# Curvature stage: fields as 32x32 products of plain float32 from turned copies of the image, with H's numerator and the step summed on TensorE

## The reference, cut to what matters

```
sobel_x, sobel_y: 3x3 kernels / 8; ux, uy = dw(u, sobel_x), dw(u, sobel_y)
uxx, uxy, uyy = dw(ux, sobel_x), dw(ux, sobel_y), dw(uy, sobel_y)     # all five clipped to +-10
g2 = ux*ux + uy*uy;  denK = 1 + g2;  denH = sqrt(1 + g2 + 1e-6)
K = clip((uxx*uyy - uxy*uxy) / (denK*denK + 1e-6), -5, 5)
H = clip(((1+uy*uy)*uxx - 2*ux*uy*uxy + (1+ux*ux)*uyy) / (2*denH**3 + 1e-6), -5, 5)
u = u + 0.01 * clip(alpha*K + beta*H, -1, 1)
u = edge-pad of u's interior                                          # ten times
return 0.7*u + 0.3*x
```

## Time and profile before

| | us |
|---|---|
| median of 3 runs (744.8 to 745.09) | 745.0 |
| the profiled execution's own time | 745.53 |
| its span, first to last instruction | 743.7 |
| PE busy | 657.2 (88%) |
| VectorE busy | 449.9 (60%) |
| ScalarE busy | 374.2 (50%) |
| GpSimd busy | 317.2 (43%) |

### The profile page before, as it was taken

How to read it: one execution, slowest core, us unless ns; L and a number is a source line. 1 busy time by engine, 2 the same in 40 slices (tenths; PEclk the granted TensorE clock), 3 DMA queues, 4 the chain that set the end, 5 groups by cost and what they waited for, 6 DMA issues and landing times.

```text
span 743.7 us, 11210 instructions
## 1 busy us (share of the span) xinstructions
PE 657.2 (88%) x4384; PEld 462.0 (62%) x4384; DVE 449.9 (60%) x673; ACT 374.2 (50%) x630; POOL 317.2 (43%) x296
## 2 busy tenths in 40 slices
PE   6997899998974566797989999999999999999994
PEld 4784774565442334454555787777777777777782
DVE  5730000095046222132444599999999999999997
ACT  1310000060000011020224699999999999999995
POOL 1000000010013100000000689999999999999993
PEclk9999999999997889899999999999999999999997
DMA  9999999999999999999982000000000000000001
GB/s 376 427 384 423 426 428 427 427 425 425 429 425 425 427 429 424 430 425 427 428 364 97 1 2 0 1 0 0 0 0 0 0 0 0 0 0 0 0 0 57
DMA packets 13347, 166.53 MB, mean 224 GB/s; under 512 B 1456, under 2 KB 1856, under 8 KB 2944
## 3 DMA queue, kind: packets, MB, share of 16 engines
q1 hardware_dynamic: 12384, 162.60, 51.7%
q0 software_dynamic: 256, 2.02, 0.7%
q10 hardware_dynamic: 672, 1.41, 0.5%
HBM read 164.98 MB, written 1.05 MB: 223 GB/s over the span
## 4 chain that ended last, share of the span: by engine, by line
DVE 39%; DMA 27%; PE 25%; issue 6%; ACT 1%; POOL 1%; DVEq 0%; POOLq 0%; SPq 0%; ACTq 0%
DMA ring<-wout_w 15%; DVE ring L905 6%; PE bank L383 6%; DVE ring L910 5%; PE bank L399 5%; DVE ring L892 4%; DVE bank L889 4%; DVE bank L925 4%; PE bank L452 4%; PE bank L507 4%; DMA ring<-wv_p 3%; DVE bank L913 3%; DMA ring<-wout_p 3%; DVE ring L916 3%; DMA ring<-wqk_p 3%
## 5 line engine op out<-in xcount | busy, mean ns | idle before, releaser
L591 PE MATMUL bank<-u_parts,vmr 128*128 128x480 f32 x1360 | 309.0, 385 | 6.6 <-DVE reg_a L899 4.7
L591 PEld LDWEIGHTS bank<-u_parts,vmr 128*128 128x128 f32 x1360 | 249.6, 188 | 65.9 <-DVE reg_a L899 16.7
L399 PE MATMUL bank<-ring,small 128*32 128x256 f32 x1152 | 76.5, 413 | 36.2 <-DMA ring<-wout_w 30.6
L399 PEld LDWEIGHTS bank<-ring,small 128*32 128x32 f32 x1152 | 38.3, 117 | 66.2 <-issue 33.0
L399 PE MATMUL bank<-ring,xw 128*32 128x256 f32 x1024 | 60.6, 394 | 13.8 <-DMA ring<-wv_w 13.8
L1144 POOL DMA_DIRECT2D vmr<-vmats x1 | 0.5, 540 | 151.3 <-PE bank L399 151.3
L1123 POOL MEMSET reg_d<- 128x2176 f32 x1 | 1.9, 1915 | 146.8 <-PE bank L459 146.8
L720 DVE SCALAR_TENSOR_TENSOR reg_a<-bank,prm 128x512 f32<-128x512 f32 x4 | 2.8, 692 | 100.9 <-PE bank L459 100.9
L383 PE MATMUL bank<-reg_a,ring 128*128 128x256 f32 x256 | 56.2, 380 | 3.0 <-DMA ring<-wqk_p 2.3
L399 PEld LDWEIGHTS bank<-ring,xw 128*32 128x32 f32 x1024 | 33.2, 113 | 39.6 <-DMA ring<-wv_w 17.1
L383 PEld LDWEIGHTS bank<-reg_a,ring 128*128 128x128 f32 x256 | 48.3, 190 | 11.1 <-DMA ring<-wqk_p 3.1
(11 more groups left out here) (197 smaller groups left out, 1026.8 us busy)
## 6 DMA issues: line engine op xcount, KB each, us to landing
ring<-wv_w SPq DMA_DIRECT2D x32, 2048.0 KB, 29.6
ring<-wout_w SPq DMA_DIRECT2D x30, 2048.0 KB, 37.0
ring<-wqk_p SPq DMA_DIRECT2D x4, 2048.0 KB, 18.9
ring<-wqk_w SPq DMA_DIRECT2D x4, 2048.0 KB, 20.7
ring<-wv_p SPq DMA_DIRECT2D x2, 2048.0 KB, 20.5
ring<-wout_p SPq DMA_DIRECT2D x2, 2048.0 KB, 22.9
ring<-wout_w SPq DMA_DIRECT2D x4, 1024.0 KB, 35.5
vmr<-vmats POOLq DMA_DIRECT2D x1, 1664.0 KB, 6.9
```

Of the source, the lines that this page charges most:

```text
L399: ins = te.matmul(bank[32 * j:32 * j + 32, b_, n0:n0 + 256], lhs(c), slot[k % NSLOT][:, c, 256 * j:256 * j + 256], start=start and c == 0, ...
L591: last = te.matmul(dst[:, 0:NF], mat(m, first), p3[:, 2 + off:S + off, :], start=(high and n == 0), stop=(not high and n == len(terms) - 1))
```

## The change

The float32r split is gone: ScalarE's high parts, GpSimd's low parts and their buffers. A term is now a plain float32 product in 32x32 tiles of the array: four matmuls, one for each row quarter, each with its own output quarter. A chunk now has its channels on quarters of 32 partitions (one channel's 32 rows), so the operator matrix is 32x32. The terms of uy, uxy and uyy/uxx read copies of the image turned by 1, 2, 3 quarters (`turned`; uxx uses the copy turned by 1), so that fields of different turns use different tiles; the output comes out in place. SyncE makes the three copies of a chunk with six DMAs, SBUF to SBUF, after every update (`turn`).

TensorE also forms sums that other engines formed: H's numerator as a + b - 2 cross (three sets of four tiles with unit and -2 matrices) and the step as alpha dt K + beta dt H (two sets). VectorE loses L925 (combining K and H) and L932 (the cross product); L905 becomes two products of 480 (K's, H's). ScalarE's joint 960-wide log and exponential are split into halves, and the Relu clips are two, not three. GpSimd forms the cross product, clips K (a tensor_scalar), and no longer makes the low part, the sum of outers or the final sum of H. TensorE's and GpSimd's programs are written out rather than looped.

The way in also changes: the first 24 columns go to HBM (eight DMAs) and back (four) in the chunk layout, and the last 8 columns are turned by 64 products with a selection matrix. `vmats` is smaller, and SyncE loads it and `select`.

```diff
-            p.dma_start(vmr[:, :], vmats).then_inc(ld_vm, 16)
+            sp.dma_start(vm[:, 0:ALPHA * S], vmats).then_inc(ld_vm, 16)
+            sp.dma_start(sel, select).then_inc(ld_sel, 16)
+            for r in range(RG):
+                sp.dma_start(to[:, :, r, :], xa4[r * C:(r + 1) * C, :, 1:1 + EARLY, :]).then_inc(st_image, 16)
+            sp.wait_ge(st_image, 16 * RG)
+            for x in range(NCH):
+                sp.dma_start(u_half(x, 0), image[x * P:(x + 1) * P, :]).then_inc(ld_u[x], 16)
+            def turn(c):
+                for t in range(1, NCH):
+                    cut_ = QUAD * t
+                    sp.dma_start(turned[cut_:P, t - 1, c, :], u[c][0:P - cut_, :]).then_inc(ld_turn[t - 1][c], 16)
+                    sp.dma_start(turned[0:cut_, t - 1, c, :], u[c][P - cut_:P, :]).then_inc(ld_turn[t - 1][c], 16)
...
+                for c in range(NCH):
+                    sp.wait_ge(po["pad"], i * NCH + (c + 1 - NCH))
+                    turn(c)
...
+            def stencil(field, c, t, first, terms, n):
+                for j in range(NCH):
+                    at_ = slice(QUAD * ((j + t) % NCH), QUAD * ((j + t) % NCH + 1))
+                    last = te.matmul(bank[QUAD * j:QUAD * (j + 1), field, 0:NF], mat(m, (j + t) % NCH), whole[at_, 2 + off:S + off, :],
...
+            def slot_step(k):
+                    if older:
+                        te.wait_ge(ve["khk"], k - 2)
+                        te.wait_ge(ve["khh"], k - 2)
+                    stencil(ux, c, 0, first, UX, 0)
+                    te.wait_ge(ld_turn[0][c], 32 * (i + 1))
+                    stencil(uy, c, 1, first, UY, 0)
+                    stencil(ux, c, 0, first, UX, 1)
+                    stencil(uy, c, 1, first, UY, 1)
+                    te.wait_ge(ld_turn[1][c], 32 * (i + 1))
+                    if old:
+                        te.wait_ge(ve["clipxy"], k - 1)
+                    stencil(uxy, c, 2, first, UXY, 0)
+                    te.wait_ge(po["clip_k"], k - 2)
+                    add(STEP, ALPHA, clip_k[q], True, False)
+                    stencil(uy, c, 1, first, UY, 2).then_inc(pe["fld1"], 1)
+                    stencil(uxy, c, 2, first, UXY, 1)
+                    te.wait_ge(ld_turn[2][c], 32 * (i + 1))
+                        te.wait_ge(ve["clip2"], k - 1)
+                    stencil(uyy, c, 3, first, UYY, 0)
+                    te.wait_ge(ac["clip_h"], k - 2)
+                    add(STEP, BETA, clip_h[q], False, True).then_inc(pe["step"], 1)
+                    stencil(uxx, c, 1, first, UXX, 0)
+                    stencil(uxy, c, 2, first, UXY, 2)
+                    stencil(uyy, c, 3, first, UYY, 1)
+                    te.wait_ge(ve["outer"], k - 1)
+                    add(h_sum, ONE, ab[n][:, 0:NF], True, False)
+                    stencil(uxx, c, 1, first, UXX, 1)
+                    stencil(uxy, c, 2, first, UXY, 3).then_inc(pe["fldxy"], 1)
+                    stencil(uyy, c, 3, first, UYY, 2)
+                    add(h_sum, ONE, ab[n][:, NF:2 * NF], False, False)
+                    stencil(uxx, c, 1, first, UXX, 2)
+                    stencil(uyy, c, 3, first, UYY, 3)
+                    te.wait_ge(po["cross"], k - 1)
+                    add(h_sum, MINUS_TWO, cross[n], False, True).then_inc(pe["hn"], 1)
+                    stencil(uyy, c, 3, first, UYY, 4).then_inc(pe["fld2"], 1)
```

VectorE's order in a slot becomes: clip1 (960, as L892), clipd (as L889) and, directly behind and dependent on it, u (as L899); khk (480), clipxy (as L913), khh (480), clip2 (960, as L910), slope (as L916), outer (960, as L920):

```diff
+                    v.wait_ge(pe["step"], k - 2)
+                    v.tensor_scalar(step, step, five_ab[:, 1:2], DT, ALU.subtract, ALU.min).then_inc(ve["clipd"], 1)
+                    v.wait_ge(ve["clipd"], k - 2)
...
-                    v.tensor_tensor(two(kh[n]), two(num[n]), fields_in(n, 0, 2), ALU.mult).then_inc(ve["kh"], 1)
+                    v.wait_ge(ac["invk"], k - 1)
+                    v.tensor_tensor(kh[n][:, 0:NF], num[n], pair(n)[:, 0, :], ALU.mult).then_inc(ve["khk"], 1)
...
+                    v.wait_ge(pe["hn"], k - 1)
+                    v.wait_ge(ac["invh"], k - 1)
+                    v.tensor_tensor(kh[n][:, NF:2 * NF], pair(n)[:, 1, :], inv_h[n], ALU.mult).then_inc(ve["khh"], 1)
```

More of the change, by code:

```diff
@@ L134 @@
 EDGE_BANK = (3, 4, 0, 1)
-NVM = 2 * len(MATS) * P
+MIXED, OUTER, STEP = 2, 3, 7
+ONE, MINUS_TWO, ALPHA, BETA = range(2 * len(MATS), 2 * len(MATS) + 4)
+NVM = (BETA + 1) * S
+TURNS = NCH - 1
+SEL = 2 * S - RG
 def build(nc, x_patch, x_window, x_conv, params, wqk_p, wv_p, wout_p, wqk_w, wv_w, wout_w,
-          conv_band, conv_halo, vmats, edge, out):
+          conv_band, conv_halo, vmats, edge, select, image, out):
     with ExitStack() as ctx:
@@ L222, in build @@
             "pl_sq_sums", "pln", "negmax", "prob", "pf", "dsl", "stage", "conv", "bank_turn", "img",
-            "clip1", "clipxy", "clip2", "slope", "outer", "cross", "kh", "diff", "clipd", "u", "scales", "fin", "halo", "u_in", "band")}
+            "clip1", "clipxy", "clip2", "slope", "outer", "khk", "khh", "clipd", "u", "scales", "mats", "fin", "halo", "u_in", "band")}
         ac = {n: sem("ac_" + n) for n in (
             "order", "patch_sq", "patch_std", "fl", "win_sq", "win_std", "pl_std", "qkv", "vt", "exp", "pt", "rows",
-            "wwk", "wv", "conv", "p2", "sqr", "sqxy", "lnw", "psq", "w15", "lnd", "inv", "end_k", "up_h", "ends", "x3", "hi", "hi_first", "halo", "u_in")}
-        po = {n: sem("po_" + n) for n in ("zero", "bandz", "pick", "padz", "lo", "lo_first", "cxy", "m", "num", "absum", "hn", "pad")}
+            "wwk", "wv", "conv", "p2", "sqr", "sqxy", "lnw", "psq", "w15", "lnk", "lnh", "invk", "invh", "low_h", "clip_h", "x3",
+            "halo", "u_in")}
+        po = {n: sem("po_" + n) for n in ("zero", "bandz", "padz", "cxy", "m", "num", "cross", "clip_k", "pad")}
+        st_image, ld_u = sem("st_image"), [sem(f"ld_u{c}") for c in range(NCH)]
+        ld_turn = [[sem(f"ld_turn{t}_{c}") for c in range(NCH)] for t in range(1, NCH)]
         ld_last, st_out = [sem(f"ld_last{n}") for n in range(NPIECE)], sem("st_out")
@@ L269, in build @@
         dual = lambda cols: [arena(cols) for _ in range(2)]
-        u_hi = [u_parts[:, c * ROWF:(c + 1) * ROWF] for c in range(NCH)]
-        u_lo = [u_parts[:, (NCH + c) * ROWF:(NCH + c + 1) * ROWF] for c in range(NCH)]
+        vm, sel = arena(NVM), arena(C * SEL)
+        turned = arena(TURNS * NCH * ROWF).rearrange("p (t c n) -> p t c n", t=TURNS, c=NCH)
         u_in = lambda c: u[c][:, B:(S + 1) * B]
         u_half = lambda c, half: u[c][:, B + early_columns(half)[0] * B:B + early_columns(half)[1] * B]
[L275 to L283, removed]
+        f01, f34, mix = dual(2 * NF), dual(2 * NF), dual(NF)
+        p2, cxy, cross, mxy, sqm, num, slope, lnw = (dual(NF) for _ in range(8))
+        ab, den, inv_h, kh = dual(2 * NF), dual(2 * NF), dual(NF), dual(2 * NF)
+        clip_k, low_h, clip_h = dual(NF), dual(NF), dual(NF)
         assert la[0] <= NSLOT * SLOTF
@@ L288, in bank_set, with pair, mat @@
             return 5 - 5 * q
[L290 to L296, removed]
+        def pair(q):
+            return bank[:, bank_set(q):bank_set(q) + 2, 0:NF]
+        def mat(n, quad):
+            return vm[quad * QUAD:(quad + 1) * QUAD, n * S:(n + 1) * S]
         def half_ready(eng, k, h):
@@ L584, in _ @@
                 ins.then_inc(pe["chunk"], 1)
[L587 to L592, removed]
-                return last
[L595 to L620, removed]
@@ L622, in _ @@
-            te.wait_ge(ld_vm, 16)
[L623 to L628, removed]
+            def stencil(field, c, t, first, terms, n):
+                off, m = terms[n]
+                m = MATS.index(m) + (0 if first else len(MATS))
+                whole = (u[c] if t == 0 else turned[:, t - 1, c, :]).rearrange("p (w b) -> p w b", b=B)
+                for j in range(NCH):
+                    at_ = slice(QUAD * ((j + t) % NCH), QUAD * ((j + t) % NCH + 1))
+                    last = te.matmul(bank[QUAD * j:QUAD * (j + 1), field, 0:NF], mat(m, (j + t) % NCH), whole[at_, 2 + off:S + off, :],
+                                     start=(n == 0), stop=(n == len(terms) - 1), skip_group_check=True)
+                return last
@@ L630, in _ @@
+            te.wait_ge(ld_vm, 16)
+            te.wait_ge(ve["mats"], 2)
+            for k in range(1, SLOTS + 2):
+                slot_step(k)
             te.wait_ge(ld_edge, 16)
             for x in range(NCH):
+                if x == NCH - 1:
+                    slot_step(SLOTS + 2)
                 if x < 2:
@@ L922, in slot_step @@
-                if old:
-                    v.wait_ge(ac["ends"], k - 1)
-                    v.scalar_tensor_tensor(mixed(n), end_k[n], ten_ab[:, 0:1], mixed(n),
-                                           ALU.min, ALU.add).then_inc(ve["diff"], 1)
-                if new:
-                    v.wait_ge(po["cxy"], k)
-                    v.wait_ge(ve["clipxy"], k)
-                    v.wait_ge(ac["sqxy"], k)
-                    v.scalar_tensor_tensor(cxy[q], cxy[q], -2.0, mixed(q), ALU.mult, ALU.mult).then_inc(ve["cross"], 1)
```

(1 more changed line is left out.)

281 lines of the change are left out of this document (117 added, 164 removed).

## The result

The changed kernel takes 727.42 us (median of 4 runs, 726.97 to 728.99) against 745.05; the ratio is 0.9766, 95% interval 0.9753 to 0.9778. It is 17.6 us faster, where 38 were forecast. The side was right. The time lies inside the whole range of 697 to 730, which had room for the rivals, and outside the forecast's own 699 to 716. The profiled execution took 728.99, the slowest of the four; its span is 727.1.

The account below looks back on a forecast made before the run. VectorE was taken to bound the kernel before and after: 428.9 us to clip1 of slot 3, 37 slots of 6.92 (256.0), 18.6 out, 1.8 around, 2 for the clock, 0.5 off for the median: 707 us, own range 699 to 716, whole 697 to 730.

Parts of the forecast that it names:

- the price of a set: TensorE: four tiles of 480 float32 columns take 0.41 us, at 0.86 ns a column.
- Loop 1: TensorE, khh to the next slot's ux and clip1: ready at 5.88 us, needed at 6.92, spare 1.0.
- rival A: TensorE: row quarters don't run side by side, 9.6 us a slot, 810 us in all; chance 0.14.
- The beat: Time of one steady slot, set by VectorE: 6.92 us against 7.91 before, bounds 6.8 to 7.15.
- The way in: Before the steady slots: clip1 of slot 3 at 428.9 us against 431.54, gain 2.6, bounds 5 and -1.
- The way out: From slot 40's clip1 to the end: 18.6 us against 19.6, 1.0 less, bounds 3 and -2.
- The 2 us for the clock: TensorE at half clock in one slot in four, 0.2 us over the beat each, charged as 2 us.
- The copies hidden: Turned image copies by DMA take 5.6 us at the most of 7.9 allowed, about 2 us to spare.
- The loops through ScalarE and GpSimd: Loops 2 and 3, through VectorE and these engines: 6.66 and 6.61 us, spare 0.3 each under the beat.
- VectorE's sum: VectorE's nine steps from start to start in a new slot add up to 6.92 us.
- Rival B: TensorE stays at half clock throughout: beat 7.11 to 7.2 us, total 712 to 717; chance 0.07.
- rival C: The turned copies come late: at a copy time of 9 us, beat 7.45 and total 727; chance 0.05.

Follow-up runs that it names:

- e3: The kernel before the change, each of 17 terms taken once as a plain float32 128x128 product instead of twice in float32r: 977.32 us.
- e6: The changed kernel with every product put on the four tiles where row quarter and column quarter agree: 1144.52 us.
- e5: The changed kernel with one TensorE wait, for khh, moved from ahead of ux's first set to in front of uy's first set: 713.14 us.
- e1: The changed kernel with the curvature stage's tiled products reading only the upper 16 bits (bfloat16) of their operands: 701.99 us.
- e2: The changed kernel without the turned copies, every product reading the unturned image: 723.0 us.
- e8: Against the changed kernel with TensorE's sets reordered and two banks exchanged (709.05 us): khk moved between clipd and u on VectorE: 718.71 us.

## Why the prediction was wrong

**The step that failed** is the price of a set. It said "six products of 512 columns in 2.84 us, and 32 of 128 columns in four column tiles", and from these 0.86 ns a column, 0.41 us a set. The rows count records. The convolution has three products at that place (dw in 0 to 2), each two records; the turning of the chunks has 16, and 32 records. The price is 1.72 ns a column by the same two equations, 0.82 a set, and e3 measures 0.81, e6 0.80. The code gave the check: 17 terms twice in 40 slots are the 1360 records of the float32r kernel, one each, and every float32 line has twice its products. Nothing else in the sum was off by so much.

**Loop 1** then reads with the prediction's own numbers 4.31+0.07+3 x 0.82+0.20+0.07 = 7.11, and it was over 6.92 already. With u's step at the measured 0.57 it is 6.98, and e5, where this loop is the one left, has 7.00. A second loop through TensorE, from khh to H's sum to khh, was worked out only under rival A. It is 0.15 to start, seven layers of 0.81 (5.67), two half layers more (0.80) in the order as written, 0.16 by which a record outlasts its 0.40, 0.03, and khh's 0.66: 7.47 in the slot above. Where in the order the two half layers go was not traced. That this loop held the beat is shown by e5: one wait moved took it to 7.00.

**The beat** was 6.92 and is 7.41: 37 x 0.493 = 18.2 us. **The way in**: clip1 of slot 3 at 433.33 and not 428.9, 4.4 us. The 64 selection products took 3.70 us in all where 0.44 a chunk was counted (the same factor), and slot 1's layers twice as long; with half the records (e1) it was 429.60. SyncE's issues have a part in it: the fourth copy was issued 2.69 us after the first (412.47 to 415.16), where 1.56 was counted. **The way out**: 19.5, not 18.6. These three make 23.5 over the forecast span of 703.5, that is 727.0; measured 727.1. The 2 us for the clock weren't spent.

**What was right.** Row quarters side by side (rival A false, e6). The copies hidden: six issues, 2.2 to 2.8 us each, and e2 gains between 1 and 4 us in the steady slots together. The loops through ScalarE and GpSimd under the beat; e8, with u inside both, has 7.15 where they add up to 7.23 and 7.18. clip_k is 0.59 (0.26 to 1.23 was the span). VectorE's sum 6.92 against 6.78 in e1: with 6.78 the forecast of 707 becomes 702, and e1 took 702. Rival B didn't occur: the granted clock was 1.00, with TensorE busy 94% of the stage.

**Luck, and two readings.** That 727 lies in the range is luck. It is what rival C gives at a copy time of 9 us, and the copies took under 3. The sign named for A and B, VectorE waiting at clip1 or khh, came, and the cause was neither. The prediction read the 34 products of the kernel before as stretched over the slot by waits. Its timeline has them in file:

```profile
607.21 6.04 PE L591 MATMUL bank<-u_parts,vmr 128*128 128x480 f32 x26 [0.17 <-DVE reg_a L899]
```

26 in 6.04 us are 0.23 each, and 34 are 7.8 of the 7.91 us, so TensorE was as near the bound as VectorE before the change. The prediction also held that a rule on different row tiles in one PSUM bank matters here only if two sets of one bank meet. But each set by itself is such a case: its four products read four row quarters and write one bank, each a quarter of it. The four records that start at 599.90 are over within 0.60, where one record takes 0.56 to 0.59, so sharing the bank didn't keep them apart.

## What to carry to other kernels

Before a record's duration becomes the price of an instruction, count the records of its line against the loop that issues them. Where an engine close to the bound works in bursts between two waits, add up the whole loop from the wait that opens it to the one that it releases: moving one wait behind one set gave 14 us here, and a new order with two banks exchanged 18. An instruction moved to cover a gap lengthens every loop that runs across its new place, as e8 shows.

## What the runs showed that was not expected

- A plain float32 product of 480 columns costs TensorE two records of 0.40 us, 0.81 in all, whether the product is 128x128 (e3) or 32x32 (e6); float32r before took one record, and bfloat16 in e1 one.
- In e1 the granted clock was 0.50 from 428 us to the end of the steady slots, with TensorE busy 103 of 200 us, and the 22 sets of a slot still fitted under VectorE's 6.78. In the changed kernel and in e2 to e8 it was 1.00 there.
- 116 GB/s of copies cost a beat held by TensorE at most 0.11 us (7.41 against 7.31 in e2, by two traces), and 0.03 by the medians.
